# Mamba and expert kernel: a float32 decay product becomes two float32r products of a split operand

## The chip, the cores and the metric

The kernel runs on one core of a Trainium2 chip. The metric is the device time of one execution in microseconds (us); the figure of a kernel is the median of its runs.

## The reference, cut to what matters

Four layers act in turn on `x` (16 sequences, 256 tokens, 128 channels, float32), each followed by a residual sum and a layer norm. The change touches the first, a Mamba block with 4 heads of 64 channels and a state of 128:

```
dt = softplus(x W_dt + dt_bias);  A = -exp(A_log);  dA = exp(dt * A)
h[t] = h[t-1] * dA[t] + dt[t] * x[t] B[t]
y[t] = h[t] C[t] + D * x[t]
```

The kernel doesn't run the recurrence step by step. It works on two chunks of 128 tokens a sequence, and needs for each pair of tokens s < t the decay between them, exp of the sum of `dt * A` over the steps from s + 1 to t. These sums are one matrix product: a strict triangle of ones times a masked copy of the step exponents `a = dt * A`. The other layers are an attention with expert-chosen values and outputs (stage b and its output part o), a linear attention (stage c), and a soft mixture of 64 experts (a second program part, `soft_experts`).

## The kernel before, in words

`token_blocks` computes the first three layers, one sequence at a time in each stage, with four stages in flight. Slot t holds stage a (Mamba) of sequence t, stage b (scores and expert values) of t - 1, stage o (expert outputs) of t - 2 and stage c of t - 3. The order of work inside a slot is written out by hand in a function `slot` of each engine (TensorE line 703, ScalarE 1032, VectorE 1436, GpSimd 1631); nothing is reordered at run time. An engine takes its instructions in that order and waits on semaphores, one per kind of event (`q["a_am"]` and so on), that count up with the sequence number. Slots t = 3 to 14 have all stages and prepare a successor; t = 0 to 2 lack some stages, and t = 15 has no successor.

What the change and the prediction touch:

- Preparation: `a_all` (line 1432), the exponents of all steps, from a chain of small VectorE operations on `sv`, `sa`, `su`, `sd`, `s2`, `sp`. TensorE, GpSimd and VectorE wait for it by counts of `prep`.
- `a_am` on GpSimd (1583): two selects a sequence, one per chunk, write `am`, the exponents of a chunk spread over 4 heads x 128 columns and zeroed below the diagonal. In slot t it runs for sequence t + 1, after `c_km` and `c_turn` and ahead of the rms root. A "root" here is `newton` (59), 15 operations on 128x2 that give a reciprocal square root; GpSimd runs one for rms (in stage a), ln1, ln2, lnB, lnC and lnD. Its order in a slot is lnB root, `a_mx`, `a_xb`, `c_km`, `c_turn`, `a_am`, rms root, `b_vg`, then the ln1, lnC, ln2 and lnD roots.
- `a_seg` on TensorE (416): the segment product, `low_s` (triangle) by `am`, 128x128 by 128x512, float32, into `ps_a`. Chunk 0 is first in the slot; then come `b_choice`, a query-key product, the gates' products `b_gates` (496), and the second `a_seg`. The profile shows a float32 product as two matrix instructions and a float32r product as one. ScalarE's `a_lx` (900) takes the exponential.
- VectorE after the gates: ScalarE's `b_eg`, then `b_gate` (1233, seven operations), `b_res`, and `a_xd` (1155), which writes `xd` and `xD`. TensorE's `a_bg` (437, first instruction on line 440) waits for them.
- `a_y` (1187): `ya` by an addition, `yg = ya * sz`; ScalarE's `a_sq` squares `yg`. `a_tz` (889, ScalarE) and `a_sz` (1143, VectorE) make the gate of z.
- `a_res` (1197, VectorE) writes `ra`; it waits for the rms root and for the output projection `a_op` (479, product on line 483). `a_ln1` (1208) starts with the two operations that write `na` (line 328) and waits for the ln1 root.
- `b_max` (1264, VectorE, tile `r`), four times a slot, feeds ScalarE's `b_probs` (962, lines 971 and 973) for two heads each; after them ScalarE's `b_rgs` writes `rgS`, and TensorE's `b_rgb` (585, line 593) transposes it.

```
            def a_seg(b, c):
                ...
                wait(pe, q["a_am"], C * b + c + 1)
                pe.matmul(ps_a[:, :], low_s[:], am[:, c, :, :].rearrange("p h t -> p (h t)"),
                          start=True, stop=True, skip_group_check=True).then_inc(q["a_seg_ps"], 1)
```

Of the kernel before, what the change touches and what calls it, by code (L numbers as in the profile page):

```python
# [5 lines left out]
F32 = mybir.dt.float32  # L6
F32R = mybir.dt.float32r
BF16 = mybir.dt.bfloat16
I32 = mybir.dt.int32
ALU = mybir.AluOpType  # L10
# [4 lines left out]
P = 128  # L15
C = L // P

NH, HD = 4, 64
DI = NH * HD
# [19 lines left out]
TT = NB * C  # L39
# [5 lines left out]
LOG1P_TERMS = 7  # L45
# [7 lines left out]
def wait(eng, sem, value):  # L53

    if not isinstance(value, int) or value > 0:
        eng.wait_ge(sem, value)
# [43 lines left out]
def token_blocks(nc, kept, x, xT, in_wT, conv_w, conv_b, dt_bias, A_log, Dh, norm_w, out_wT, ln_w, ln_b,  # L100
# [5 lines left out]
    with ExitStack() as ctx:  # L106
        def sb(name, shape, dt=F32):
            return ctx.enter_context(nc.sbuf_tensor(name, [P] + shape, dt))
# [9 lines left out]
        negb_f = sb("negb_f", [3, P])  # L118
        negb = sb("negb", [3, P], BF16)
        low_s = sb("low_s", [P])  # L120
        upp_s = sb("upp_s", [P])
        hof = sb("hof", [P])
        hof_n = sb("hof_n", [P])
# [41 lines left out]
        bet = sb("bet", [D])  # L165


        sv = sb("sv", [TT, NH])
        sa = sb("sa", [TT, NH])
        su = sb("su", [TT, NH])  # L170
        sd = sb("sd", [TT, NH])
        s2 = sb("s2", [TT, NH])
        sp = sb("sp", [TT, NH])
        ea = sb("ea", [NH])
        dt_all = sb("dt_all", [TT, NH])
        a_all = sb("a_all", [TT, NH])


        xt_in = sb("xt_in", [2, L])
# [5 lines left out]
        xD = sb("xD", [C, NH, HD])  # L185
        btok = sb("btok", [P])
        gm = sb("gm", [C, P])
        am = sb("am", [C, NH, P])
        lx = sb("lx", [C, NH, P])
        mx = sb("mx", [C, NH, P])  # L190
        ep = sb("ep", [NH])
        xst = sb("xst", [NH, HD])
        st = sb("st", [DI])
        inter = sb("inter", [NH, HD])
        tz = sb("tz", [C, DI])
        sz = sb("sz", [C, DI])
        ya = sb("ya", [C, DI])
        yg = sb("yg", [C, DI])
        sq = sb("sq", [DI])
        ssq = sb("ssq", [C])  # L200
        yT = sb("yT", [2, L])
# [59 lines left out]
        ps_a = ctx.enter_context(nc.psum_tensor("ps_a", [P, 512], F32))  # L261
# [5 lines left out]
        prep = sem("prep")  # L267
# [24 lines left out]
        COLS = [(bq_s, bq), (bk_s, bk)]  # L292
        READY = 16 * (len(CONSTS) + len(ROWS) + len(COLS))
        SOFT = 16
        PREP = SOFT + LOG1P_TERMS + 11
        PREP_ACT = 7

        def wait_both(eng, *waits):

# [88 lines left out]
        def _(pe):  # L388
# [27 lines left out]
            def a_seg(b, c):  # L416

                if c == 0:
                    wait(pe, q["a_sz"], b + 1)
                    wait(pe, q["a_x1h"], b)  # L420
                    wait(pe, q["a_x1l"], b)
                else:
                    wait(pe, q["a_lx"], C * b + 1)
                wait(pe, q["a_am"], C * b + c + 1)
                pe.matmul(ps_a[:, :], low_s[:], am[:, c, :, :].rearrange("p h t -> p (h t)"),
                          start=True, stop=True, skip_group_check=True).then_inc(q["a_seg_ps"], 1)

            def a_xt(b):
                wait(pe, q["a_xbc"], b + 1)
# [441 lines left out]
        def _(act):  # L871
            def copy(dst, src):
                return nc.scalar.activation(dst, src, ACT.Copy)  # L873
# [14 lines left out]

            def a_tz(b):
                wait(act, q["a_z_ps"], b + 1)  # L890
                wait(act, q["a_sz"], b)
                nc.scalar.activation(tz[:].rearrange("p c n -> p (c n)"), ps_a[:], ACT.Tanh, scale=0.5
                                     ).then_inc(q["a_tz"], 1)

# [131 lines left out]
            copy(wgH[:], wg_f[:]).then_inc(prep_act, 1)  # L1026
            nc.scalar.activation(ea[:], alog[:], ACT.Exp).then_inc(prep_act, 1)
            copy(id_r[:], id_f[:]).then_inc(prep_act, 1)
            act.wait_ge(prep, SOFT + 2)
            nc.scalar.activation(su[:], sa[:], ACT.Exp, scale=-1.0).then_inc(prep_act, 1)  # L1030

# [94 lines left out]
        def _(dve):  # L1126
# [16 lines left out]
            def a_sz(b):  # L1143

                wait(dve, q["a_tz"], b + 1)
                wait(dve, q["a_yg"], b)
                V.scalar_tensor_tensor(sz[:].rearrange("p c n -> p (c n)"), tz[:].rearrange("p c n -> p (c n)"), 1.0,
                                       ps_a[:], ALU.add, ALU.mult).then_inc(q["a_sz"], 1)

# [36 lines left out]

            def a_y(b):
                wait(dve, q["a_y_ps"], b + 1)
                wait(dve, q["a_int"], 2 * b + 2)
                V.tensor_tensor(ya[:].rearrange("p c n -> p (c n)"), ps_a[:], xD[:].rearrange("p c h d -> p (c h d)"),  # L1190
                                ALU.add).then_inc(q["a_y"], 1)
                wait(dve, q["a_y"], b + 1)
                wait(dve, q["a_sq"], C * b)
                wait(dve, q["a_yt_ps"], b)
                V.tensor_tensor(yg[:], ya[:], sz[:], ALU.mult).then_inc(q["a_yg"], 1)

            def a_res(b, u):
# [223 lines left out]
            for k in range(LOG1P_TERMS - 1, 0, -1):  # L1421
# [10 lines left out]
            V.scalar_tensor_tensor(a_all[:], dt_all[:], -1.0, ea[:].unsqueeze(1).to_broadcast([P, TT, NH]),  # L1432
                                   ALU.mult, ALU.mult).then_inc(prep, 1)
            dve.wait_ge(prep, SOFT + at + 4)

            def slot(r, u, a, b, o, c, more):
                t = 2 * r + u
# [142 lines left out]
        def _(pool):  # L1580
            G = nc.gpsimd

            def a_am(b):

                for c in range(C):
                    wait(pool, q["a_seg_ps"], C * b)
                    G.affine_select(out=am[:, c, :, :], in_=a_all[:, b * C + c, :].unsqueeze(2).to_broadcast([P, NH, P]),
                                    compare_op=ALU.is_ge, fill=0.0, base=0, pattern=[[0, NH], [1, P]],
                                    channel_multiplier=-1).then_inc(q["a_am"], 1)

            def a_mx(b):

# [33 lines left out]
                G.tensor_scalar(kmh[:], h16[:], km[:], None, ALU.mult).then_inc(q["c_km"], 1)  # L1626

            pool.wait_ge(ready, READY)
            pool.wait_ge(prep, SOFT + LOG1P_TERMS + 10)

            def slot(r, u, a, b, o, c, more):
                t = 2 * r + u
# [666 lines left out]
```

## Time and profile before

| | |
|---|---|
| Runs | 1599.06, 1599.17, 1600.42 us; median 1599.17 |
| Profiled execution | 1601.12 us |
| Its span (first to last instruction) | 1599.2 us |
| Granted TensorE clock, mean | 0.969 |
| TensorE matrix products busy | 1442.7 us, 90% |
| Weight loads busy | 1262.2 us, 79% |
| VectorE busy | 1209.4 us, 76% |
| ScalarE busy | 820.1 us, 51% |
| GpSimd busy | 796.9 us, 50% |

The profile names the engines PE (TensorE; PEld its weight loads), DVE (VectorE), ACT (ScalarE) and POOL (GpSimd). Busy shares are of the whole span. Products are pipelined and their ends are modelled, so the busy share of PE says little of how hard it works. The 16 slots of `token_blocks` run from 34 us to some 965 us; `soft_experts` fills the time from 1095 us to the end. The mean clock is below 1 because of short stretches at a lower granted clock early and between the two parts.

### The profile page before, as it was taken

The page shows a single profiled execution, that of the slowest core. Times are in us where ns is not written, and L with a number is a line of the kernel's source. Part 1 is how long each engine was busy: PE and PEld are TensorE (multiplying, and loading weights), DVE is VectorE, ACT ScalarE, POOL GpSimd, SP SyncE. Part 2 cuts the span into 40 slices and gives each one's busy share as a digit, 9 for nine tenths or more (in the row PEclk, how much of TensorE's full clock was granted, in tenths as well). Part 3 has the DMA queues.
Part 4 walks back from the last instruction along what each step waited for, and adds up shares of the span by engine and source line. Part 5 has one row for each costly group of instructions (what it writes and reads, how often), then busy time and mean ns, then how long its engine had stood idle before and what let it go on. Part 6 is the DMA issues. An engine that isn't in the chain of part 4 may idle for free. (4 is left out here: it accounts for less than half of the span.)

```text
span 1599.2 us, 32323 instructions
## 1 busy us (share of the span) xinstructions
PE 1442.7 (90%) x10752; PEld 1262.2 (79%) x10752; DVE 1209.4 (76%) x2290; ACT 820.1 (51%) x1846; POOL 796.9 (50%) x2004
## 2 busy tenths in 40 slices
PE   5588999999999999999999999754999999869997
PEld 4366788788888788887888877543999999869997
DVE  4466798898898898898898887533888888827664
ACT  2234544544544545545445443202676777557775
POOL 0332253563563463463563552233777777657763
PEclk9997999999999999999999999866999999989999
DMA  6000000000000000000000000006677766867782
GB/s 233 7 7 1 8 1 14 15 1 14 15 1 14 14 2 14 15 1 14 15 1 14 8 5 5 7 7 207 177 197 197 191 184 191 265 245 302 302 323 70
DMA packets 140752, 132.10 MB, mean 83 GB/s; under 512 B 7376, under 2 KB 130512, under 8 KB 134096
## 3 DMA queue, kind: packets, MB, share of 16 engines
q1 hardware_dynamic: 140624, 130.50, 25.9%
q8 instruction: 68, 1.11, 0.3%
q14 instruction: 60, 0.49, 0.1%
HBM read 73.85 MB, written 56.62 MB: 82 GB/s over the span
## 5 line engine op out<-in xcount | busy, mean ns | idle before, releaser
L622 PE MATMUL bk<-ve_f,oe 128*128 128x128 f32 x2048 | 277.0, 279 | 2.6 <-DVE ve_f L1300 2.6
L622 PEld LDWEIGHTS bk<-ve_f,oe 128*128 128x128 f32 x2048 | 249.7, 192 | 25.9 <-issue 20.7
L1300 DVE SCALAR_TENSOR_TENSOR ve_f<-ps_m,oT 128x512 f32<-128x512 f32 x256 | 171.8, 679 | 5.2 <-PE bk L622 3.4
L2187 POOL TENSOR_TENSOR d_s<-d_ex 128x1024 f32<-128x1024 f32 x32 | 131.8, 4120 | 87.1 <-ACT d_ex L1987 87.1
L1261 DVE COPY_PREDICATED vals<-oh,bk 128x1024 f32<-128x1024 int32 x112 | 146.6, 1309 | 10.6 <-PE bk L393 8.8
L1937 PE MATMUL d_sl<-d_ex,e_prT 128*128 128x128 f32 x1024 | 135.8, 276 | 9.4 <-POOL d_ex L2204 9.4
L1871 PE MATMUL d_lg<-d_phf,d_xtf 128*128 (+1 forms) x1024 | 125.0, 282 | 15.9 <-DMA d_xtf<-x_T 6.8
L1871 PEld LDWEIGHTS d_lg<-d_phf,d_xtf 128*128 128x128 f32 x1024 | 122.0, 199 | 16.8 <-issue 7.1
L1937 PEld LDWEIGHTS d_sl<-d_ex,e_prT 128*128 128x128 f32 x1024 | 125.2, 193 | 9.7 <-POOL d_ex L2204 9.7
L1881 PE MATMUL d_sl<-d_ex,d_xs 128*128 128x128 f32 x1024 | 121.4, 277 | 5.7 <-DVE d_ex L2102 5.7
L1881 PEld LDWEIGHTS d_sl<-d_ex,d_xs 128*128 128x128 f32 x1024 | 118.5, 194 | 6.1 <-DVE d_ex L2102 6.1
L971 ACT ACTIVATE ve_f<-bk,r 128x128 f32<-128x128 f32 x128 | 47.2, 369 | 137.0 <-DVE r L1273 136.8
L391 PE MATMUL bk<-veH,x1H 128*128 128x512 f32 x256 | 115.4, 451 | 0.9 <-DVE vals L1261 0.8
L2084 DVE TENSOR_REDUCE d_nm<-d_lg 128x128 f32<-128x2048 f32 x32 | 73.3, 2290 | 49.1 <-PE d_lg L1871 44.0
L63 POOL TENSOR_SCALAR lnB_v<-lnB_mv 128x2 f32<-128x2 f32 x16 | 3.1, 192 | 213.6 <-DVE lnB_mv L317 213.6
L873 ACT ACTIVATE pt<-bk 128x384 f32<-128x384 f32 x128 | 62.5, 494 | 75.0 <-PE bk L563 73.7
L393 PE MATMUL bk<-veH,x1L 128*128 128x512 f32 x256 | 100.7, 393 | 0.0
L392 PE MATMUL bk<-veL,x1H 128*128 128x512 f32 x256 | 100.5, 392 | 0.0
L2039 ACT ACTIVATE e_prT<-d_lg 128x512 f32<-128x512 f32 x128 | 72.4, 594 | 47.9 <-PE d_lg L1924 47.9
L2204 POOL TENSOR_TENSOR d_ex<-d_ex,e_bias 128x1024 f32<-128x1024 f32 x32 | 74.9, 2362 | 40.2 <-DMA d_ex<-y_slots 40.2
L1140 DVE SCALAR_TENSOR_TENSOR cacc<-cin,cw,cacc 128x256 f32<-128x256 f32 x192 | 86.3, 494 | 3.1 <-ACT cin L873 3.0
L1982 ACT ACTIVATE d_raw<-d_lg 128x512 f32<-128x512 f32 x128 | 71.5, 602 | 33.3 <-PE d_lg L1871 16.5
(283 smaller groups left out, 3733.4 us busy)
## 6 DMA issues: line engine op xcount, KB each, us to landing
logits<-d_raw SPq DMA_DIRECT2D x128, 256.0 KB, 3.3
e_lt<-logits SPq DMA_DIRECT2D x32, 1024.0 KB, 5.6
y_slots<-d_ys SPq DMA_DIRECT2D x64, 256.0 KB, 4.3
d_ex<-y_slots SPq DMA_DIRECT2D x16, 1024.0 KB, 7.3
d_w<-W SPq DMA_DIRECT2D x16, 256.0 KB, 3.4
oe<-xT SPq DMA_DIRECT2D x1, 2048.0 KB, 7.8
xt_in<-xT SPq DMA_DIRECT2D x16, 128.0 KB, 2.3
x_in<-x SPq DMA_DIRECT2D x16, 128.0 KB, 2.4
```

The lines of the kernel that those rows point to most:

```text
L391: pe.matmul(ps, lh, rh, start=first, stop=False, skip_group_check=True)
L392: pe.matmul(ps, lh, rl, start=False, stop=False, skip_group_check=True)
L393: return pe.matmul(ps, ll, rh, start=False, stop=last, skip_group_check=True)
L622: last = pe.matmul(ps_u[:, cols], oe[:, hp, e, :], mo[:, n % MO, hp, :], start=False, stop=(e == NE - 1 and hp == HP - 1), skip_group_chec ...
L1140: V.scalar_tensor_tensor(cacc[:, ch, :], cin[:, ch, tap:tap + L], cw[:, ch, tap:tap + 1], cacc[:, ch, :], ALU.mult, ALU.add).then_inc(q["a ...
L1261: V.copy_predicated(vals[:], oh[:, :, :, e:e + 1].bitcast(I32).to_broadcast([P, C, HB, DH]), ps_v[e % 2][:].rearrange("p c (h k) -> p c h ...
L1300: V.scalar_tensor_tensor(mo[:, n % MO, :, :].rearrange("p a n -> p (a n)"), ps_m[:], float(NE - e), oT[:, u, c, :, :].rearrange("p a n -> ...
L1871: last = pe.matmul(lg[:, k, i, :], xtf[:, b, c, :], phf[:, cols], start=(i == 0), stop=(i == BB - 1), skip_group_check=True)
L1881: last = pe.matmul(sl[:, k, i, :], xs[:, (BK * i + k) * C + c, :], ex[:, u, c, k, i, :], start=(c == 0 and i == 0), stop=(c == C - 1), ski ...
L1937: last = pe.matmul(po[:, c, :], prT[:, c, s, :], yb[:, v, s, :], start=(s == 0), stop=(s == SB - 1), skip_group_check=True)
L2187: G.tensor_tensor(s8[:], part[:, 0:8, :], part[:, 8:16, :], ALU.add).then_inc(n, 1)
L2204: G.tensor_tensor(yb[:, v, rows, :], yb[:, v, rows, :], bias[:, rows, :], ALU.add).then_inc(e["y"], 1)
```

## The change

The exponents are split once, in the preparation: `aH` is `a_all` rounded to float32r, `aL` the rest. Both are masked by selects on GpSimd, into `amH` and `amL`, four selects a sequence instead of two. The segment product becomes two float32r products that add up in PSUM, with a triangle `low_r` that ScalarE copies to float32r once. To make room, the six small tiles of the preparation lie on `lx`, `sz` lies on `tz` and `yg` on `ya`, and the waits that guard these tiles move accordingly. The counts of preparation events go up by two (VectorE) and one (ScalarE).

```diff
@@ tiles @@
+        low_r = sb("low_r", [P], F32R)
...
-        sv = sb("sv", [TT, NH])
-        sa = sb("sa", [TT, NH])
-        su = sb("su", [TT, NH])
-        sd = sb("sd", [TT, NH])
-        s2 = sb("s2", [TT, NH])
-        sp = sb("sp", [TT, NH])
+        aH = sb("aH", [TT, NH], F32R)
+        aL = sb("aL", [TT, NH], F32R)
...
-        am = sb("am", [C, NH, P])
+        amH = sb("amH", [C, NH, P], F32R)
+        amL = sb("amL", [C, NH, P], F32R)
         lx = sb("lx", [C, NH, P])
         mx = sb("mx", [C, NH, P])
+        sv, sa, su, sd, s2, sp = (lx[:, :, :, :].rearrange("p c h t -> p (c h t)")[:, TT * NH * i:TT * NH * (i + 1)]
+                                  .rearrange("p (n h) -> p n h", h=NH) for i in range(6))
...
-        sz = sb("sz", [C, DI])
+        sz = tz
         ya = sb("ya", [C, DI])
-        yg = sb("yg", [C, DI])
+        yg = ya
@@ counts @@
-        PREP = SOFT + LOG1P_TERMS + 11
-        PREP_ACT = 7
+        PREP = SOFT + LOG1P_TERMS + 13
+        PREP_ACT = 8
@@ TensorE, a_seg @@
-                pe.matmul(ps_a[:, :], low_s[:], am[:, c, :, :].rearrange("p h t -> p (h t)"),
-                          start=True, stop=True, skip_group_check=True).then_inc(q["a_seg_ps"], 1)
+                pe.matmul(ps_a[:, :], low_r[:], amH[:, c, :, :].rearrange("p h t -> p (h t)"),
+                          start=True, stop=False, skip_group_check=True)
+                pe.matmul(ps_a[:, :], low_r[:], amL[:, c, :, :].rearrange("p h t -> p (h t)"),
+                          start=False, stop=True, skip_group_check=True).then_inc(q["a_seg_ps"], 1)
@@ ScalarE, a_tz @@
-                wait(act, q["a_sz"], b)
+                wait(act, q["a_yg"], b)
@@ ScalarE, preparation @@
             copy(id_r[:], id_f[:]).then_inc(prep_act, 1)
+            copy(low_r[:], low_s[:]).then_inc(prep_act, 1)
@@ VectorE, a_sz @@
-                wait(dve, q["a_yg"], b)
@@ VectorE, a_y @@
                 wait(dve, q["a_y_ps"], b + 1)
+                wait(dve, q["a_sq"], C * b)
+                wait(dve, q["a_yt_ps"], b)
                 wait(dve, q["a_int"], 2 * b + 2)
...
                 wait(dve, q["a_y"], b + 1)
-                wait(dve, q["a_sq"], C * b)
-                wait(dve, q["a_yt_ps"], b)
@@ VectorE, preparation, behind a_all @@
             dve.wait_ge(prep, SOFT + at + 4)
+            V.tensor_copy(aH[:], a_all[:]).then_inc(prep, 1)
+            dve.wait_ge(prep, SOFT + at + 5)
+            V.tensor_tensor(aL[:], a_all[:], aH[:].bitcast(F32), ALU.subtract).then_inc(prep, 1)
+            dve.wait_ge(prep, SOFT + at + 6)
@@ GpSimd, a_am @@
                 for c in range(C):
                     wait(pool, q["a_seg_ps"], C * b)
-                    G.affine_select(out=am[:, c, :, :], in_=a_all[:, b * C + c, :].unsqueeze(2).to_broadcast([P, NH, P]),
-                                    compare_op=ALU.is_ge, fill=0.0, base=0, pattern=[[0, NH], [1, P]],
-                                    channel_multiplier=-1).then_inc(q["a_am"], 1)
+                    for part, whole in ((amH, aH), (amL, aL)):
+                        ins = G.affine_select(out=part[:, c, :, :], in_=whole[:, b * C + c, :].bitcast(F32)
+                                              .unsqueeze(2).to_broadcast([P, NH, P]),
+                                              compare_op=ALU.is_ge, fill=0.0, base=0, pattern=[[0, NH], [1, P]],
+                                              channel_multiplier=-1)
+                    ins.then_inc(q["a_am"], 1)
@@ GpSimd, start @@
-            pool.wait_ge(prep, SOFT + LOG1P_TERMS + 10)
+            pool.wait_ge(prep, SOFT + LOG1P_TERMS + 12)
```

## Rows read from the trace of the kernel before

**Rows 1.** Busy time by stretch: start:end, length, each engine's busy time, granted clock, DMA.

```profile
core 0: us, PE busy (x) PEld busy (x) DVE busy (x) ACT busy (x) POOL busy (x), PEclk, DMA share, GB/s
...
123.00:144.00 21.00, 17.17 (x81) 9.93 (x79) 10.45 (x29) 9.11 (x29) 3.18 (x15) 0.59 0.00 1
200.00:900.00 700.00, 680.98 (x4880) 567.23 (x4879) 612.77 (x1419) 351.40 (x986) 354.00 (x1200) 1.00 0.03 10
```

**Rows 2.** Waits, whole span: who waited for whom, total us, times, longest us.

```profile
DVE ra L1203 <- PE ps_a L483: 14.3, 15, 5.3
...
PE ps_o L593 <- ACT rgS L873: 15.1, 18, 1.4
```

**Rows 3.** Timeline, 553 to 559: start, us, engine, line, operation, tiles, shapes, count, idle before.

```profile
553.58 0.28 PE L393 MATMUL ps_o<-wgH,x1L 128*128 128x64 f32 x1
...
553.70 1.10 PE L425 MATMUL ps_a<-am,low_s 128*128 128x512 f32 x2
...
554.21 0.23 DVE L1238 TENSOR_SCALAR eg<-eg 128x128 f32<-128x128 f32 x1 [2.29 <-ACT eg L943]
...
557.67 0.40 PE L392 MATMUL bk<-veL,x1H 128*128 128x512 f32 x1
...
557.91 0.39 PE L393 MATMUL bk<-veH,x1L 128*128 128x512 f32 x1
...
558.15 0.68 DVE L1161 TENSOR_TENSOR xD<-ps_a,d_h 128x512 f32<-128x512 f32 x1
...
558.88 0.14 PEld L440 LDWEIGHTS ps_a<-id_f,xbc 128*128 128x128 f32 x1 [0.32 <-DVE xD L1161]
```

**Rows 4.** Timeline, 575 to 590, and `ra` in the first and last slot of twelve.

```profile
575.89 1.22 POOL L1587 TENSOR_SCALAR_AFFINE_SELECT am<-a_all 128x512 f32<-128x512 f32 x2
...
581.88 1.06 PE L483 MATMUL ps_a<-out_w,yT 128*128 128x128 f32 x8
...
582.46 0.20 POOL L76 TENSOR_TENSOR rms_y<-rms_y,rms_t 128x2 f32<-128x2 f32 x1
...
582.60 2.05 POOL L1604 TENSOR_TENSOR vals<-vals,gx 128x512 f32<-128x512 f32 x2
...
583.04 0.61 DVE L1203 SCALAR_TENSOR_TENSOR ra<-ps_a,rms_y,x_in 128x128 f32<-128x128 f32 x2 [0.67 <-PE ps_a L483]
...
588.51 0.65 PE L577 MATMUL ps_o<-pt,vals 128*64 128x256 f32 x4
...
588.95 0.19 POOL L76 TENSOR_TENSOR ln_y<-ln_y,ln_t 128x2 f32<-128x2 f32 x1
...
589.29 0.61 DVE L328 TENSOR_SCALAR na<-ra,ln_mv,ln_y 128x128 f32<-128x128 f32 x2
...
228.28 0.61 DVE L1203 SCALAR_TENSOR_TENSOR ra<-ps_a,rms_y,x_in 128x128 f32<-128x128 f32 x2 [0.67 <-PE ps_a L483]
...
878.21 0.61 DVE L1203 SCALAR_TENSOR_TENSOR ra<-ps_a,rms_y,x_in 128x128 f32<-128x128 f32 x2 [0.67 <-PE ps_a L483]
```

**Rows 5.** VectorE from `ra` to `b_max` (a stretch), then the timeline, 600 to 610.

```profile
583.04:601.99 18.95, 18.36 (x58) 1.00 0.01 2
...
600.85 0.95 DVE L1270 TENSOR_REDUCE r<-bk 128x6 f32<-128x768 f32 x1
...
604.10 0.44 PE L593 MATMUL ps_o<-id_f,rgS 128*128 128x128 f32 x2 [0.82 <-ACT rgS L873]
...
609.93 1.12 PE L425 MATMUL ps_a<-am,low_s 128*128 128x512 f32 x2
```

**Rows 6.** Timeline at the kernel's start, and the second segment product of t = 1.

```profile
28.88 0.29 DVE L1432 SCALAR_TENSOR_TENSOR a_all<-dt_all,ea 128x128 f32<-128x128 f32 x1
...
29.20 3.21 DVE L1140 SCALAR_TENSOR_TENSOR cacc<-cin,cw,cacc 128x256 f32<-128x256 f32 x6
...
29.32 1.63 POOL L1587 TENSOR_SCALAR_AFFINE_SELECT am<-a_all 128x512 f32<-128x512 f32 x2 [28.81 <-DVE a_all L1432]
...
33.59 0.69 DVE L1147 SCALAR_TENSOR_TENSOR sz<-tz,ps_a 128x512 f32<-128x512 f32 x1 [1.18 <-ACT tz L892]
...
88.13 2.06 PE L425 MATMUL ps_a<-am,low_s 128*128 128x512 f32 x2
```

## The prediction

> **What bounds the kernel now.** I read the stretches first. From 200 to 900 us, the part in which the changed code runs in its steady form, TensorE is busy for 681 of 700 us at a granted clock of 1.00 and VectorE for 613 [rows 1]. That looks like a TensorE bound. The list of waits says otherwise: two waits come back slot after slot. VectorE waits for the output projection before `ra` (15 times), and TensorE waits for ScalarE's `rgS` before the transposes of L593 (18 times) [rows 2]. So I followed one slot to its end at 609.93, where the next one's first segment product starts.
>
> Its order is this. Behind the first segment product, the gates' last product runs at 553.58, the second segment product at 553.70, VectorE's gate chain starts at 554.21 and goes on without a mark of idle time to `xD`, which ends at 558.83; TensorE's weight load for `a_bg` comes 0.05 us after that and had waited 0.32 us for it [rows 3]. From there the work passes through VectorE and ScalarE to GpSimd, which does `km`, `t2`, the two selects (575.89 to 577.11) and then the 15 small operations of the rms root, which end at 582.66. VectorE's `ra` starts at 583.04, released by TensorE's L483, which ended at 582.94. GpSimd goes straight on, and its ln1 root ends at 589.14, 0.15 us before VectorE's `na` [rows 4]. From `ra` to the fourth `b_max`, whose reduction ends at 601.80, no row of VectorE carries a mark of idle time: the window from 583.04 to 601.99 has 18.36 us busy out of 18.95, and 58 instructions share the small gaps that are left [rows 5]. ScalarE's last two heads hang on that `b_max`, then `rgS`, then TensorE, which had stood still for 0.82 us at 604.10; after it TensorE runs to the next slot [rows 5]. The loop is a ring: TensorE at the slot's start, VectorE, ScalarE, GpSimd, VectorE, ScalarE, TensorE. GpSimd's rms root has only 0.38 us to spare in it (582.66 to 583.04), its ln1 root 0.15 us (589.14 to 589.29), the time of the signal included.
>
> **The change part by part.**
> *Segment products.* A float32 128x512 product is two instructions, and takes 1.10 us by the record; counted from the end of the gates' product (553.86) to its own (554.80) it holds the array for 0.94 us. A float32r product of the same size follows the one before after 0.24 us (557.67, 557.91) [rows 3]. Two of them: 0.47 us, so 0.47 us less a product, 32 products.
> *Which of the two counts.* The first one stands ahead of the gates, so gates, gate chain, `xD`, and all behind it come 0.47 us earlier. The second stands beside the gate chain: TensorE gets to `a_bg` earlier and waits there for `xD`, which it already follows by 0.05 us [rows 3]. I take 0 for it, at most 0.05 us.
> *Masks.* Each slot that prepares a successor gets two more selects. The pair took 1.22 us here [rows 4], and 1.63 us at the kernel's start, beside VectorE's taps of the convolution [rows 6]. The trace has no select with a float32r output; I take 1.22 us for the new pair, nearest in place and form, and keep 1.63 us as the upper end. At the lower end the pair takes 1.22 us too, and half of VectorE's 0.59 us of small gaps swallows 0.3 us of it. Queued behind the selects on GpSimd: rms root, `b_vg`, ln1, lnC, ln2, lnD roots, all 1.22 us later. `b_vg` ends at 584.65 and is read by L577 at 588.51, 3.9 us later [rows 4], so it stays hidden; the lnC, ln2 and lnD roots follow the ln1 root and are wanted in the same order by a VectorE that is then as late as they are. The rms and ln1 roots have 0.38 and 0.15 us.
> *So per steady slot:* the ring up to GpSimd gains 0.47; `ra` moves by -0.47 + 1.22 - 0.38 = +0.37, `na` by -0.47 + 1.22 - 0.15 = **+0.60 us**. VectorE has nothing idle to take that up before the fourth `b_max`; TensorE's stop at L593 grows with it, and the next slot starts 0.60 us late. `ra` waits for L483 by 0.67 us in the first slot of this kind (228.28) and the last (878.21) [rows 4]; these are 12 slots, t = 3 to 14: +7.2 us.
> *Other slots.* At t = 0, 1 and 2 stage c doesn't run, GpSimd isn't held up by it ahead of the selects, and I take them as free. At t = 0 both products are hidden (ScalarE's copy of the experts, VectorE's subtraction of it). At t = 1 TensorE runs at half rate although the granted clock reads 1.00: the second product took 2.06 us [rows 6]. TensorE sets the pace there; two products save up to 1.0 us each, of which I keep 1.5 us in all. At t = 2 the first is again at half rate: 1.0 us. t = 15 has no selects: 0.5 us. Together -3.0 us, between -1.5 and -4.
> *Preparation.* VectorE gets a copy and a subtraction of 128x128 before the first taps: some 0.55 us, by 0.29 us for the product that makes `a_all`. The cover is the 1.18 us in which it waits for `tz` before `sz` at 33.59; without it they would cost 0.55 us once. The first selects start at 29.9 instead of 29.32 and take up to 3.3 us instead of 1.63: done at 33.2, before `sz` ends at 34.28 and lets the first segment product go [rows 6]. ScalarE's copy of `low_r` falls into its wait for VectorE. All 0.
> *Buffers.* `sz` on `tz`, `yg` on `ya`: the waits that move are on events of the slot before or of work already waited for; the copies keep their sizes. `sv` to `sp` on `lx` are dead before `lx` is written. 0.
>
> **Sum:** +7.2 - 3.0 = +4.2 us. It is made in the profiled execution (1601.12 us, span 1599.2), which stands 2 us above the median of the runs, 1599.17; I carry the difference over to the median: **1603.4 us**. With the bounds: +0.3 (gaps swallowed) to +1.01 a slot (pair of 1.63), so +3.6 - 4 = -0.4 to +12.1 - 1.5 = +10.6: 1598.8 to 1609.8. A measurement of this kernel can't tell less than 0.2% (3.2 us) from no change.
>
> One rule speaks against this change. The rows: 1.63 us for the first pair of selects beside the taps of the convolution (29.20 to 32.41, from SBUF to SBUF), 1.22 us for the pair in the steady slot [rows 4, 6]. The Trainium skill, SBUF — State Buffer, section "SBUF: two separate sides", says that VectorE with two SBUF inputs and a reading GpSimd operation exclude each other for a whole instruction; the trace agrees. By it a new pair that meets such taps would take 1.63 us each time, and the sum would be +12.1 - 3.0 = +9.1 us, 1608.3 us. I keep 1.22 us, because whatever the new pair meets, the root's operations, which stand in its place now, no longer meet.
>
> **The rivals.**
> *A. TensorE is the bound* (busy 97% [rows 1]). Then both products count in every slot: 32 x 0.47 = 15.0 us, and 1.4 us more for the three at half rate: 1582.8 us. For it: the busy share. Against it: the stop at L593 in every slot, and VectorE's unbroken work ahead of it. [...] 0.08.
> *B. The selects are absorbed* on the way, in GpSimd or in VectorE's small gaps, and the first product alone counts: 13 x 0.47 + 2.5 = 8.6 us off: 1590.6 us. For it: 18.95 less 18.36 us of small gaps. Against: they are the latencies of a serial chain. 0.14.
> *C. Slower by more.* The place is `na` at GpSimd's ln1 root, the price is the new pair's time less 0.15 us, and it comes fully if the float32r products are no shorter than float32 ones (the change does not do what it says): 12 x 1.07 = +12.8 us, 1612.0 us. It decides from the point where the pair's time less what the first product saves is over 0.15 us; in my forecast it is 0.75. For it nothing but the long pair; against it the 0.24 us between float32r products. 0.10.
> *D. The clock.* From 123 to 144 us the granted clock is 0.59 on the mean [rows 1], around slots in which TensorE waits often; if its fall or rise moves, that is a few us either way. 0.06.
>
> **How the numbers follow.** Forecast 0.62. Of it 0.48 lies above +3.2 us and 0.14 within it. Faster: A, B and a little of D, 0.23; same 0.15; slower 0.48 + C + rest of D = 0.62. The range leaves out A, half of B's spread, half of C and a bit of D, under 0.2: 1590 to 1611 us. The forecast's own range is 1598.8 to 1609.8.
>
> **What would show it.** L425's products: 64 records at about 0.4 us, spaced 0.24. GpSimd's selects: 64. `ra` in the steady slots released by GpSimd's `rms_y`, no longer by L483; `na` by `ln_y`. TensorE's stop at L593 grows from 0.82 us, and new ones appear at `a_bg`. The steady slot: 0.6 us longer. It is wrong if the period falls, or if `ra` is still released by TensorE. The part after 1095 us must not change in length.

## The result, and the profile after

The changed kernel took 1607.61 us (median of 8 runs, 1605.15 to 1611.61) against 1600.91 us for the kernel before on the same chip (8 runs, 1598.27 to 1602.51). The ratio is 1.0048, with a 95% interval of 1.0037 to 1.0059: slower by 6.7 us by the medians, by 7.7 us by the ratio. The forecast was 1603.4 us and slower, with a range of 1590 to 1611 us. The changed kernel's profiled execution took 1607.86 us, its span is 1606.0 us.

All lines below L425 have moved down a little: L483 is now L485, L593 is L595, `ra` is L1205, the selects are L1594. First the busy times of the whole span, then the stretches that [rows 1] show for the kernel before, both of the changed kernel:

```profile
PE 1435.4 (89%) x10752; PEld 1265.0 (79%) x10752; DVE 1220.5 (76%) x2292; ACT 817.3 (51%) x1847; POOL 815.0 (51%) x2036
```

```profile
core 0: us, PE busy (x) PEld busy (x) DVE busy (x) ACT busy (x) POOL busy (x), PEclk, DMA share, GB/s
123.00:144.00 21.00, 15.58 (x86) 10.63 (x87) 11.43 (x31) 10.46 (x33) 3.16 (x15) 0.76 0.00 1
200.00:900.00 700.00, 670.48 (x4816) 560.57 (x4816) 617.60 (x1399) 344.59 (x973) 361.63 (x1205) 1.00 0.03 10
```

From 200 to 900 us TensorE is busy for 10.5 us less than before, GpSimd for 7.6 us and VectorE for 4.8 us more. TensorE got its shorter work and stands still more. The list of waits of the changed kernel says where (who waited for whom, total us, times, longest):

```profile
PE ps_o L595 <- ACT rgS L875: 17.3, 18, 2.1
...
PE ps_c L668 <- DVE qr L1337: 13.1, 15, 1.5
...
PEld ps_a L442 <- DVE xD L1163: 10.6, 14, 2.5
...
DVE ra L1205 <- POOL rms_y L76: 8.5, 12, 0.7
...
DVE ra L1205 <- PE ps_a L485: 7.2, 3, 5.3
```

The first is the wait of [rows 2], grown from 15.1 us. The second is new among the long waits, and the third, 6.0 us in the kernel before, has taken in part of what the second product saves. VectorE's wait of `ra` for the output projection, 15 times and 14.3 us before [rows 2], is left in 3 slots; in the other 12 `ra` now waits for GpSimd's `rms_y`. One steady slot, t = 9, shows it (timeline of the changed kernel: start, us, engine, line, operation, idle before):

```profile
554.42 0.50 PE L425 MATMUL ps_a<-amH,low_r 128*128 128x512 f32 x1
...
554.75 0.39 PE L427 MATMUL ps_a<-amL,low_r 128*128 128x512 f32 x1
...
579.01 0.63 POOL L1594 TENSOR_SCALAR_AFFINE_SELECT amH<-aH 128x512 fp32r<-128x512 f32 x1
...
580.77 0.82 POOL L1594 TENSOR_SCALAR_AFFINE_SELECT amL<-aL 128x512 fp32r<-128x512 f32 x1
581.67 0.24 POOL L63 TENSOR_SCALAR rms_v<-ssq 128x2 f32<-128x2 f32 x1
...
586.64 0.20 POOL L76 TENSOR_TENSOR rms_y<-rms_y,rms_t 128x2 f32<-128x2 f32 x1
586.79 2.04 POOL L1613 TENSOR_TENSOR vals<-vals,gx 128x512 f32<-128x512 f32 x2
...
586.87 0.61 DVE L1205 SCALAR_TENSOR_TENSOR ra<-ps_a,rms_y,x_in 128x128 f32<-128x128 f32 x2 [0.71 <-POOL rms_y L76]
...
588.33 0.53 DVE L1285 TENSOR_TENSOR rg<-rg,gx 128x4 f32<-128x4 f32 x1
...
593.48 0.61 DVE L328 TENSOR_SCALAR na<-ra,ln_mv,ln_y 128x128 f32<-128x128 f32 x2
...
608.25 0.44 PE L595 MATMUL ps_o<-id_f,rgS 128*128 128x128 f32 x2 [0.97 <-ACT rgS L875]
...
614.09 0.50 PE L425 MATMUL ps_a<-amH,low_r 128*128 128x512 f32 x1
```

The way to read this is to count everything from the slot's first segment product. Here that is 554.42, and the next slot's is 614.09: a period of 59.67 us. In the kernel before it is 59.03 us, which puts the start of the slot of [rows 5] at 609.93 - 59.03 = 550.90. So `ra` starts at 32.45 here (586.87 - 554.42) and at 32.14 before (583.04 - 550.90); the rms root ends at 32.42 and at 31.76; `na` starts at 39.06 and at 38.39. `ra` is now released by GpSimd's `rms_y`, no longer by TensorE. From `ra` to `na` it was 6.25 us and is 6.61.

Two rows of VectorE and one of GpSimd in the kernel before, for what has changed length:

```profile
577.04 0.87 DVE L1140 SCALAR_TENSOR_TENSOR cacc<-cin,cw,cacc 128x256 f32<-128x256 f32 x2
...
584.50 0.17 DVE L1283 TENSOR_TENSOR rg<-rg,gx 128x4 f32<-128x4 f32 x1
```

```profile
577.19 0.37 POOL L63 TENSOR_SCALAR rms_v<-ssq 128x2 f32<-128x2 f32 x1
```

The product of the first two heads' gates, L1283 before and L1285 after, has 4 columns, and took 0.17 us before and 0.53 after. In the kernel before GpSimd's product of the same tiles (L1604, [rows 4]) was just ending, at 584.65. It now runs in the middle of it: L1613 began at 586.79 and lasted 2.04 us, to 588.83; L1285 ends at 588.86. The same pair of taps of the convolution (L1140, now L1143) took 0.87 us at 577.04 before and, beside the third and fourth select, 1.70 after:

```profile
580.16 1.70 DVE L1143 SCALAR_TENSOR_TENSOR cacc<-cin,cw,cacc 128x256 f32<-128x256 f32 x2
...
582.50 0.69 DVE L1337 TENSOR_TENSOR qr<-ve_f,wq_f 128x512 f32<-128x512 f32 x1
```

`qr` comes behind those taps, and that is TensorE's new wait at L668. With the selects moved away from there (below) this wait is back to 2 times and 2.5 us, as in the kernel before.

### The profile page after: what moved, and what is told of

Same layout as the page of the kernel before. It is cut to its first block and busy times, and to the rows that moved or that the text cites. A ratio compares the mean times of both kernels' runs of the same rounds, so it can differ in the third digit from the quotient of the medians.

```text
span 1606.0 us, 32343 instructions
## 1 busy us (share of the span) xinstructions
PE 1435.4 (89%) x10752; PEld 1265.0 (79%) x10752; DVE 1220.5 (76%) x2292; ACT 817.3 (51%) x1847; POOL 815.0 (51%) x2036
## 5 line engine op out<-in xcount | busy, mean ns | idle before, releaser
L63 POOL TENSOR_SCALAR lnB_v<-lnB_mv 128x2 f32<-128x2 f32 x16 | 3.1, 192 | 208.1 <-DVE lnB_mv L317 208.1
L1143 DVE SCALAR_TENSOR_TENSOR cacc<-cin,cw,cacc 128x256 f32<-128x256 f32 x192 | 97.0, 549 | 3.1 <-ACT cin L875 3.0
```

The source lines that it names most:

```text
L1143: V.scalar_tensor_tensor(cacc[:, ch, :], cin[:, ch, tap:tap + L], cw[:, ch, tap:tap + 1], cacc[:, ch, :], ALU.mult, ALU.add).then_inc(q["a ...
```

## The experiments

**Theory.** GpSimd is in the ring: the two added selects stand ahead of the rms root, `ra` and `na` wait for that, and this outweighs the shorter first product. **Rivals.** The shared tiles, the moved waits or the split in the preparation cost the time; the float32r pair is no shorter; TensorE is the bound; or the selects slow VectorE wherever they are. Each run has a time, a ratio to the kernel before on the same chip, and the period of t = 9. Each median is over 5 to 12 runs.

| kernel | median us | ratio (95%) | period | `ra` | `na` | `ra` released by |
|---|---|---|---|---|---|---|
| before | 1600.9 | 1 | 59.03 | 32.14 | 38.39 | TensorE L483 |
| changed | 1607.6 | 1.0048 (1.0037 to 1.0059) | 59.67 | 32.45 | 39.06 | GpSimd `rms_y` |
| two selects, pair | 1595.9 | 0.9961 (0.9946 to 0.9976) | 58.63 | 31.74 | 37.99 | TensorE L485 |
| four selects, whole product | 1611.1 | 1.0058 (1.0041 to 1.0074) | 60.11 | 32.91 | 39.52 | GpSimd `rms_y` |
| changed, selects early | 1594.7 | 0.9958 (0.9942 to 0.9975) | 58.64 | 31.74 | 38.00 | TensorE L485 |
| before, selects early | 1599.5 | 0.9995 (0.9984 to 1.0005) | 59.03 | 32.14 | 38.40 | TensorE L483 |
| tiles and preparation only | 1599.8 | 1.0002 (0.9991 to 1.0013) | 59.03 | 32.13 | 38.39 | TensorE L483 |
| early, chunk 0 whole | 1601.2 | 1.0010 (1.0001 to 1.0019) | 59.05 | 32.15 | 38.42 | TensorE L490 |
| early, chunk 1 whole | 1595.4 | 0.9969 (0.9957 to 0.9980) | 58.67 | 31.77 | 38.04 | TensorE L490 |
| gate of one operand | 1607.8 | 1.0053 (1.0039 to 1.0067) | 59.70 | 32.47 | 39.09 | GpSimd `rms_y` |
| changed, gates first | 1610.4 | 1.0064 (1.0046 to 1.0082) | 59.82 | 32.50 | 39.21 | GpSimd `rms_y` |
| early, gates first | 1596.5 | 0.9972 (0.9963 to 0.9982) | 58.74 | 32.16 | 38.14 | own queue |
| early, one single pass | 1592.8 | 0.9947 (0.9932 to 0.9963) | 58.40 | 31.51 | 37.78 | TensorE L483 |
| changed, once more | 1608.1 | 1.0045 (1.0030 to 1.0060) | 59.72 | 32.50 | 39.12 | GpSimd `rms_y` |

The columns `ra` and `na` are their starts, counted from the slot's first segment product.

### Two selects and the pair of products

Both passes read the masked rounded part, so the low part of the decay is left out of the sum.

```diff
-                    for part, whole in ((amH, aH), (amL, aL)):
+                    for part, whole in ((amH, aH),):
...
-                pe.matmul(ps_a[:, :], low_r[:], amL[:, c, :, :].rearrange("p h t -> p (h t)"),
+                pe.matmul(ps_a[:, :], low_r[:], amH[:, c, :, :].rearrange("p h t -> p (h t)"),
```

> The two single passes as in the changed kernel, but both read the masked rounded part, so that only two selects stand in the ring (the low part of the decay is left out of the sum). GpSimd ring theory: the selects are the whole price; the rms root ends 1.22 us earlier in each block than in the changed kernel (about 31.2 after the block's first product), the first residual is again released by the transposes of L483, and the period is 59.03 - 0.40 = 58.6: about 1595 us, 0.996 of before. Rival, buffers and order (shared tiles, the queries' wait at TensorE, the rotated values): the period stays near 59.6, about 1607. Rival, TensorE is the bound: the float32r pair saves all it can, 1591 or less.

1595.85 us, period 58.63. The timeline of its t = 9:

```profile
578.72 0.61 DVE L1205 SCALAR_TENSOR_TENSOR ra<-ps_a,rms_y,x_in 128x128 f32<-128x128 f32 x2 [0.67 <-PE ps_a L485]
```

The wait of `ra` is again TensorE's, and again 0.67 us. With the added selects gone and all else of the change in place, the kernel is 0.4% faster than before. It is not the shared tiles, and not 1591 us or less, which a TensorE bound would give.

### Four selects and one whole product

```diff
-                pe.matmul(ps_a[:, :], low_r[:], amH[:, c, :, :].rearrange("p h t -> p (h t)"),
-                          start=True, stop=False, skip_group_check=True)
-                pe.matmul(ps_a[:, :], low_r[:], amL[:, c, :, :].rearrange("p h t -> p (h t)"),
-                          start=False, stop=True, skip_group_check=True).then_inc(q["a_seg_ps"], 1)
+                pe.matmul(ps_a[:, :], low_s[:], amH[:, c, :, :].rearrange("p h t -> p (h t)"),
+                          start=True, stop=True, skip_group_check=True).then_inc(q["a_seg_ps"], 1)
```

```diff
-                    for part, whole in ((amH, aH), (amL, aL)):
+                    for part, whole in ((amL, aL), (amH, a_all)):
```

The selects stay four, of which those of the low part are read by nothing; `amH` holds the whole exponents.

> Four selects as in the changed kernel, but the product is one float32 product of the whole exponents again. GpSimd ring theory: the rms root goes later by the 0.40 us that the first product gives, 32.8 after the block's first product, period 60.06, some 12 x 0.4 = 5 us over the changed kernel: 1612, 1.007 of before. Rival, TensorE is the bound: 32 products of 0.40 more, 1620. Rival, the pair of products is itself the trouble (its start, its wait): 1601, as before.

1611.06 us, period 60.11. This is the price of the selects without the gain: 60.11 - 59.03 = 1.08 us a slot. The changed kernel lies 0.44 us a slot below it.

```profile
588.93 0.61 DVE L1203 SCALAR_TENSOR_TENSOR ra<-ps_a,rms_y,x_in 128x128 f32<-128x128 f32 x2 [0.72 <-POOL rms_y L76]
```

### The selects early, in the changed kernel and in the kernel before

```diff
+                if more:
+                    a_am(t + 1)
                 if c:
                     c_km(t - 3)
                     c_turn(t - 3)
-                if more:
-                    a_am(t + 1)
```

> The changed kernel with the next block's four selects put on GpSimd ahead of the key moments of stage three (L1633) and of the product with the cosines, where the engine waits some 8 us for the gelu, instead of behind them. GpSimd ring theory: the rms root is no longer behind the selects, the first residual is released by TensorE (L483), and the first product's 0.40 us comes through: period 58.6, 1607.6 - 12 x 1.03 = 1595 us, 0.996 of before. Rival, port: beside other VectorE work the selects cost it as much again, and 1 to 3 us less comes back. Rival, buffers and order: stays at 1607.

> The same move of the two selects in the kernel before. GpSimd ring theory: the rms root had 0.38 us to spare there, TensorE's transposes of L483 released the first residual, so the move gives nothing: 1600.9 +- 1.5, period 59.03. Rival, the root was the bound in the kernel before too (the transposes only recorded as last): the period falls by up to 1.2 us and the time by up to 14.

The changed kernel with this move took 1594.69 us, the kernel before with it 1599.54. GpSimd of the first, in t = 9 (the slot starts at 545.10):

```profile
559.01 0.83 POOL L1594 TENSOR_SCALAR_AFFINE_SELECT amH<-aH 128x512 fp32r<-128x512 f32 x1
...
560.97 0.64 POOL L1594 TENSOR_SCALAR_AFFINE_SELECT amL<-aL 128x512 fp32r<-128x512 f32 x1
567.66 0.42 POOL L1633 TENSOR_SCALAR km<-ks 128x1 f32<-128x1 f32 x1 [6.06 <-ACT wk_f L1013]
...
575.02 0.29 POOL L76 TENSOR_TENSOR rms_y<-rms_y,rms_t 128x2 f32<-128x2 f32 x1
```

```profile
576.84 0.61 DVE L1205 SCALAR_TENSOR_TENSOR ra<-ps_a,rms_y,x_in 128x128 f32<-128x128 f32 x2 [0.67 <-PE ps_a L485]
...
583.10 0.59 DVE L328 TENSOR_SCALAR na<-ra,ln_mv,ln_y 128x128 f32<-128x128 f32 x2
```

The four selects now lie in a time in which GpSimd waited for ScalarE anyway; the wait before `km` is still 6.06 us long, where the changed kernel has 8.61. The rms root ends at 575.31, 1.53 us ahead of `ra`. The period is 58.64, and this version beats both kernels: 0.42% below the kernel before. In the kernel before the same move does nothing that can be measured, so its root was not the bound, and the whole of what the move gives the changed kernel is the price of the added selects. What the selects cost VectorE in their new place doesn't reach the ring.

### Shared tiles and preparation alone

Two selects of `a_all` into `amH` and one float32 product of it; `sz` on `tz`, `yg` on `ya`, `sv` to `sp` on `lx`, the moved waits, `aH`, `aL` and `low_r` stay.

```diff
-                    for part, whole in ((amH, aH), (amL, aL)):
+                    for part, whole in ((amH, a_all),):
```

> Only the shared tiles (sz on tz, yg on ya, the softplus tiles on lx), the moved waits and the split in the preparation are left of the change; the ring has two selects of the whole exponents and one float32 product again. GpSimd ring theory: period 59.03 and the time of before, 1600.9 +- 1.5, with some 0.3 us more ahead of the first product. Rival, the shared tiles cost: anything over 1602, with a later L1188/L1196 or tanh L894 and a period above 59.1.

1599.8 us, period 59.03, `ra` released by L483 with the old 0.67 us. These parts cost nothing, as the prediction had it.

### Which of the two products counts

On the version with early selects, the product of one chunk is made whole again, from a select of `a_all` into a tile of its own (`amF`). This select takes the place of the one of `aL`; the one of `aH` stays and is read by nothing, so a sequence has four selects as before:

```diff
+                if c == 0:
+                    pe.matmul(ps_a[:, :], low_s[:], amF[:, :, :].rearrange("p h t -> p (h t)"),
+                              start=True, stop=True, skip_group_check=True).then_inc(q["a_seg_ps"], 1)
+                    return
```

and for chunk 1 with `if c == 1:`.

> On the version with early selects: the product of chunk 0 alone is one float32 product of whole exponents (one select for it). My step says that the first product of a block is in the ring and the second is not: period up from 58.63 to 59.03, 13 x 0.40 = 5 us over that version, about 1600. Rival, both products or neither sit in the ring: +2.6 for each half of it, or 0.

> The same for chunk 1 alone. My step says that this product has cover (TensorE waits behind it at L442 for the product with D): period 58.63 as in the version with early selects, 1594.7 +- 1.5, and the wait at L442 shorter by some 0.2 us at most. Rival, TensorE bound: 16 x 0.40 = 6 us more, 1601; a mixed case: the wait of L442 (0.19) is used up first and 0.2 us of each block shows, 1597.

Chunk 0 whole: period 59.05, 1601.2 us. Chunk 1 whole: period 58.67, 1595.4 us. Against 58.64 the first product carries 0.41 us and the second 0.03. Both slots stand as predicted; the first kernel's time is 6.5 us over the version with early selects where 13 x 0.40 = 5.2 was expected. The two ran on different chips; by the ratios, each to the kernel before on its own chip, it is 8.3 us, and the two intervals together reach down to 4.2. The timeline of the second kernel shows the cover used up: TensorE's transpose at `a_bg` comes without an idle mark, where the changed kernel has 0.19, and so has the version with early selects (552.68).

```profile
552.33 0.33 PE L447 MATMUL ps_a<-id_f,xbc 128*128 128x128 f32 x1
```

```profile
562.00 0.33 PE L442 MATMUL ps_a<-id_f,xbc 128*128 128x128 f32 x1 [0.19 <-DVE xD L1163]
```

The first row is of the kernel with chunk 1 whole, the second of the changed kernel.

### One single pass alone

Early selects, one pass, two selects; the low part of the decay is left out of the sum.

```diff
-                    for part, whole in ((amH, aH), (amL, aL)):
+                    for part, whole in ((amH, aH),):
...
-                          start=True, stop=False, skip_group_check=True)
-                pe.matmul(ps_a[:, :], low_r[:], amL[:, c, :, :].rearrange("p h t -> p (h t)"),
-                          start=False, stop=True, skip_group_check=True).then_inc(q["a_seg_ps"], 1)
+                          start=True, stop=True, skip_group_check=True).then_inc(q["a_seg_ps"], 1)
```

> Early selects, with one single pass of the rounded part alone (the low part of the decay left out, two selects, 32 of 64 products). It prices one single pass in the ring: a whole product recorded 0.94, the pair about 0.5. Theory: the ring starts with the first product, so the period falls by one pass, about 0.24 us, to 58.4: 3 us off 1594.7, about 1591.8. Rival, the first product no longer in the ring once the selects are early: 1594.7.

1592.78 us, period 58.40: 0.24 us less for one pass less. A pass in the ring costs what the records of [rows 3] space them by. The pair saved 0.40 us and not 0.47. The start of the first segment product and of TensorE's next product, in the kernel before and then in the changed one:

```profile
550.91 1.13 PE L425 MATMUL ps_a<-am,low_s 128*128 128x512 f32 x2
551.97 0.39 PE L605 MATMUL ps_m<-ohT,pick 64*128 64x128 bf16 x4
```

```profile
555.08 0.39 PE L607 MATMUL ps_m<-ohT,pick 64*128 64x128 bf16 x4
```

The whole product takes 1.06 us (550.91 to 551.97) and the pair 0.66 (554.42 to 555.08). The prediction had 0.94 and 0.47. A pair is more than two spacings of 0.24 us, since its first pass takes 0.33 (554.42 to 554.75).

### What holds `na`: three tries

In the changed kernel `na` moved by 0.67 us and `ra` by 0.31. First, L1285 of the first two heads with one operand (their gate is left out, they keep the plain reciprocal):

```diff
+                if hp == 0:
+                    V.tensor_scalar(rg[:, :, heads], rg[:, :, heads], 1.0, None, ALU.mult).then_inc(n, 1)
```

> The changed kernel, with the product of the first two heads' gates (L1285, 128x4, two operands in SBUF) done as a product of one operand with 1.0; the gate of these heads is left out. It took 0.53 us there beside GpSimd's L1613 and 0.17 in the kernel before, and na (L328) was late by 0.66 where ra was late by 0.31. Port theory: the operation falls to 0.17, na starts some 0.1 us earlier and now waits for the ln1 root, which leaves a period of 59.55, about 1606. Rival, GpSimd's root alone times na: the operation stays at 0.5, or falls and na does not move, 1607.6.

1607.77 us, and the operation took as long with one operand as with two. VectorE and GpSimd of this kernel:

```profile
585.29 0.53 DVE L1286 TENSOR_SCALAR rg<-rg 128x4 f32<-128x4 f32 x1
```

```profile
583.75 2.04 POOL L1616 TENSOR_TENSOR vals<-vals,gx 128x512 f32<-128x512 f32 x2
```

It ends at 585.82, GpSimd's product at 585.79. The experiment did not take the hold away, so it doesn't decide. It fits a lock that this form asks for too: the Trainium skill, SBUF — State Buffer, section "SBUF: two separate sides", names VectorE's two-port modes beside two SBUF inputs. Second, the gates are put ahead of `ra`:

```diff
+                if b:
+                    b_rg(t - 1, 0)
                 if a:
                     a_res(t, u)
-                if b:
-                    b_rg(t - 1, 0)
```

> The changed kernel with the reciprocal and the product of the first two heads' gates (L1283, L1285) issued on VectorE ahead of the first residual ra instead of behind it, where VectorE idles 0.71 us anyway and GpSimd's L1613 has not begun. Theory: in the changed kernel L1285 is held to the end of L1613 (0.53 us instead of 0.17) and VectorE's own work, not the ln1 root, times na (6.61 us from ra to na, 6.26 in the kernel before). With the gates ahead L1285 takes 0.17, ra to na falls to the root's bound (38.91 + 0.04 after the first product, from 39.06), period 59.55, about 1606. Rival, na waits for the root alone: na stays at 39.06 and the period at 59.66.

> Early selects and the gates ahead of ra as well. Theory, VectorE's work between ra and na is the ring there (the ln1 root ends 0.40 ahead of na): 0.35 us of it moves into the 0.67 us in which VectorE waits for ra's product, so na comes at 37.65 instead of 38.01 and the period falls from 58.63 to 58.28: 4 us off 1594.7, about 1590.5. Rival, another wait takes over at once (TensorE's own work, the kr copy, the rgS turn): period 58.6, 1594.7.

Neither came out. In the changed kernel L1285 is down to 0.17 us, but the period rose to 59.82. VectorE and then GpSimd:

```profile
584.54 0.17 DVE L1285 TENSOR_TENSOR rg<-rg,gx 128x4 f32<-128x4 f32 x1
...
587.44 0.42 DVE L1354 TENSOR_TENSOR rc<-rc,x 128x256 f32<-128x256 f32 x1
...
591.85 0.35 DVE L328 TENSOR_SCALAR na<-ra,ln_mv,ln_y 128x128 f32<-128x128 f32 x1 [0.68 <-POOL ln_y L76]
```

```profile
587.46 0.48 POOL L65 TENSOR_SCALAR ln_h<-ln_v 128x2 f32<-128x2 f32 x1
```

VectorE reaches `na` early and waits 0.68 us for the ln1 root, whose L65 took 0.48 us beside VectorE's `rc`, where it takes 0.22 in the changed kernel (589.19). The root ends 0.27 us later in the slot (39.18 against 38.91). So both bounds, VectorE's own work and the root, lie within 0.15 us of each other, and moving one operation makes the engines meet elsewhere. With early selects the gates meet GpSimd's L1613 (GpSimd, then VectorE):

```profile
575.49 2.04 POOL L1613 TENSOR_TENSOR vals<-vals,gx 128x512 f32<-128x512 f32 x2
```

```profile
576.49 1.06 DVE L1285 TENSOR_TENSOR rg<-rg,gx 128x4 f32<-128x4 f32 x1
577.48 0.60 DVE L1205 SCALAR_TENSOR_TENSOR ra<-ps_a,rms_y,x_in 128x128 f32<-128x128 f32 x2
```

L1285 lasts until 577.55, L1613 until 577.53. It lies ahead of `ra` there and puts it off by 0.42 us (32.16 against 31.74); 58.74 instead of the hoped-for 58.28. The gates stay where they were.

### The changed kernel once more

> The changed kernel once more, for the blocks ahead of the steady stretch (t = 1 and t = 2, 54.32 and 58.10 us in its first profile, where the granted clock fell to 0.50). If these two follow the clock and not the change, they come out differently here, by over 0.5 us each, with another granted clock from 104 to 150 us, and the steady period stays at 59.66; if they are the change's, they repeat within 0.2.

The steady slots repeat: 59.68 to 59.75 from t = 3 to t = 12. t = 1 and t = 2 don't: 52.83 and 54.85 us here, 54.32 and 58.10 in the first profile, 55.54 and 56.75 in the kernel before. The granted clock differs with them. The same window as in [rows 1]:

```profile
core 0: us, PE busy (x) PEld busy (x) DVE busy (x) ACT busy (x) POOL busy (x), PEclk, DMA share, GB/s
123.00:144.00 21.00, 16.90 (x101) 11.34 (x102) 12.31 (x32) 12.17 (x35) 2.55 (x11) 0.80 0.01 1
```

Two executions of one kernel are 4.8 us apart by the start of t = 3 (191.62 and 196.43 us).

## Why the prediction was right, and where its sum was off

*The ring.* Right. The changed kernel is slower because GpSimd's selects stand between VectorE's work and the rms root. Taking the added selects away or out of that place turns 1.0048 into 0.9961 or 0.9958; adding them without the shorter products gives 1.0058; the rest of the change alone gives 1.0002. Of the signs, the period rose and `ra` is released by `rms_y`. One did not come: `na` was to be released by `ln_y`, and its row carries no mark of idle time.

*The first product.* Predicted -0.47 us, measured -0.40 (the root's neighbours in the frame, and 59.03 to 58.63 in the first experiment). The second product: predicted 0, measured 0.03 of its 0.4.

*The masks.* Predicted 1.22 us for the new pair. From the first select to the root's first operation it was 577.19 - 575.89 = 1.30 us and is 581.67 - 579.01 = 2.66 us: 1.36 more, since the fourth select took 0.82. But the root behind them takes 5.17 us (581.67 to 586.84) where it took 5.47 (577.19 to 582.66 [rows 4]). Net 1.06 us. That it is shorter because it meets other work of VectorE is the trade named as the reason for keeping 1.22 instead of 1.63; it fits single rows such as that of L63 (0.37 us before, 0.24 after), but no run isolates it. The price of 1.63 by the port rule, 1608.3 us in sum, is close to the time measured, but the steady slot doesn't bear it out: it would have given 12.1 us and gave 7.7.

*`ra`.* Predicted +0.37, measured +0.31. *`na`.* Predicted +0.60, measured +0.67, and the period +0.64: over the twelve slots, 12 x 0.64 = 7.7 us against 7.2 (read directly, from the start of t = 3 to that of t = 15, 708.9 us before and 716.6 after: 7.6). The size is right, one step under it is not. The prediction gave the ln1 root 0.15 us to spare and let it set `na`. In the kernel before it was VectorE's own queue that set `na`: with its selects early the root ended at 37.98 in the slot, 0.42 us ahead of `na`, and `na` stayed at 38.40; in the changed kernel the root and VectorE's queue reach it within 0.15 us, and the queue is later because L1285 was held for 0.36 us, to the end of GpSimd's L1613. The root alone, ending at 38.91, would have put `na` at 38.95 or so, +0.56 (an estimate, which no run isolates). So what set `na` was VectorE's queue, with a hold that the prediction didn't foresee; that it gives nearly the shift of the root (+0.67 and +0.56) is luck. The lock was weighed in the prediction for the selects alone, and not for the work that the selects push `ra` into.

*The other slots.* This is the term whose size failed: -3.0 us predicted. By the medians the whole is +6.7 us, of which the steady slots make 7.6 to 7.7, so about -1 us is left for all else. The 0.5 us of t = 15 came nearly whole. Its first segment product starts at 905.10 in the kernel before and at 912.99 in the changed one, so `ra` is at 30.41 before and at 29.97 after:

```profile
935.51 0.61 DVE L1203 SCALAR_TENSOR_TENSOR ra<-ps_a,rms_y,x_in 128x128 f32<-128x128 f32 x2 [0.53 <-PE ps_a L483]
```

```profile
942.96 0.61 DVE L1205 SCALAR_TENSOR_TENSOR ra<-ps_a,rms_y,x_in 128x128 f32<-128x128 f32 x2 [0.53 <-PE ps_a L485]
```

The last store of `token_blocks` is still 0.46 us nearer to that product (183.66 and 183.20 us behind it). The 2.5 us of t = 1 and 2 can't be found. Together the two slots took 112.3 us in the kernel before, 112.4 and 107.7 in the changed kernel's two profiles. In the four profiles with both products whole they took 108.2 to 112.3 us, mean 110.2; in the seven with both as pairs 107.7 to 112.4, mean 109.7. The scatter goes along with the granted clock: in the five profiles with a mean of 0.89 from 104 to 150 us the two slots took 107.7 to 109.0 us, in the nine with 0.78 to 0.85 108.7 to 112.4. What the pair saves in them stays open. Without these 2.5 us the sum would have been 1605.9 us.

*The rivals.* A is out: a TensorE busy 97% of the stretch was not the bound. The Trainium skill, Perfetto Trace Analysis, section "Identifying the Most-Contended Engine", judges TensorE's headroom not by the busy share of its products but by its arithmetic rate and the busy share of its weight loads. This trace agrees that the products' share misleads: the weight loads were busy for 81% of the stretch (567.23 of 700 us), less than VectorE's 88% [rows 1], and TensorE's shorter work went with a longer period. B is out: the selects were not absorbed, 1.06 of 1.36 us came through. C is out: the float32r pair is shorter. D is no explanation of the difference, which stands in slots at a granted clock of 1.00. The part behind `token_blocks` (from 1095 us in the kernel before), which the change doesn't touch, took 504.2 us from its first product to the end in the kernel before, and 503.5 and 505.1 us in the changed kernel's two profiles, so it adds scatter and no difference that can be told.

*Tiles, preparation.* 0 was right. The first segment product came at 34.63, 0.29 us later than in the kernel before (34.34). t = 0 got 0.16 us of that back (49.38 us instead of 49.54); the other 0.1 us is too little to be seen in the time.

## What to carry to other kernels

When a change trades TensorE's work for some on another engine, count both in one frame, from the loop's first instruction, on the ring and not by busy share; here 0.40 us came off and 1.06 us went on. Then ask whether the added work has another place on its own engine: the same instructions in front of a wait of 8.6 us cost nothing, and a loss of 0.5% became a gain of 0.4%. A term read from a stretch whose clock varies from one execution to the next doesn't belong in the sum, only in the range.

## What the runs showed of the hardware that was not expected

- VectorE and GpSimd hold each other up down to the smallest operations. A product of 128x4 took 0.17 us with GpSimd's L1613 not yet begun and 0.53 or 1.06 us in the middle of it, each time until that one's end; a GpSimd operation of 128x2 took 0.48 us instead of 0.22 beside a VectorE product of 128x256. So each move of one of them shifts the other by some tenths of a us.
- The hold came for a multiplication with one operand as well (0.53 us), and not for the reciprocal of the same size just before it (0.16 us, 588.14 to 588.30 in the changed kernel, while L1613 ran).
- One float32r pass of 128x512 costs 0.23 to 0.24 us in the ring, the first of a pair 0.33; a float32 product of that size 0.40 us more than the pair (1.06 and 0.66 us to the start of the next product).
